# Two Fourier layers on one core: four splits in a row, image halves waited for apart, raw loads by ScalarE

## The reference

```
x = x + L0(gn(x))      # rfft2, keep 16x16 modes, mix channels per mode, irfft2; plus gn(x) @ skip + bias
x = x + L1(gn(x))      # rfft2, keep 32x32 modes, mix with fw1 and fw2, irfft2 = out; relu(out @ W + b + out)
```

## Time and profile before

| | |
|---|---|
| median of 3 runs | 2583.09 us (2573.79 to 2587.32) |
| profiled execution, its own time | 2586.72 us |
| its span | 2584.9 us |
| its mean granted clock of TensorE | 0.836 |
| busy, share of the span | TensorE 74%, VectorE 55%, ScalarE 44%, GpSimd 8% |
| bytes moved by DMA | 590.30 MB, mean 228 GB/s |

### The profile page before, as it was taken

One profiled execution on the slowest core, in us unless ns is written; L12 is line 12 of the kernel. 1 busy time (PEld: TensorE's weight loads), 2 busy tenths in 40 slices (PEclk: granted clock), 3 DMA queues, 4 the chain that ended last, 5 costly groups with the idle time before them and its releaser, 6 DMA issues. The chain is left out here.

```text
span 2584.9 us, 60445 instructions
## 1 busy us (share of the span) xinstructions
PE 1920.0 (74%) x24234; PEld 1537.6 (59%) x24234; DVE 1411.0 (55%) x2087; ACT 1145.1 (44%) x1884; POOL 194.5 (8%) x218
## 2 busy tenths in 40 slices
PE   4788887888389233323453699989999989999999
PEld 3566665667357232323343577777877777777877
DVE  5665665664144300000352576677777767777876
ACT  4544454553023200000232565556666556555665
POOL 0000000000100310110001120200102020201000
PEclk9999998999555555555676899999999999999999
DMA  7777676772664999999654487887878788878887
GB/s 274 237 221 221 222 229 204 231 238 87 153 83 67 193 232 232 233 234 223 168 179 176 130 285 261 286 287 238 279 255 302 257 288 271 294 267 266 275 285 274
DMA packets 239409, 590.30 MB, mean 228 GB/s; under 512 B 67302, under 2 KB 159938, under 8 KB 202306
## 3 DMA queue, kind: packets, MB, share of 16 engines
q1 hardware_dynamic: 203266, 570.90, 74.1%
q10 hardware_dynamic: 35072, 12.59, 2.4%
q0 software_dynamic: 768, 2.56, 0.3%
HBM read 380.99 MB, written 168.30 MB: 212 GB/s over the span
## 5 line engine op out<-in xcount | busy, mean ns | idle before, releaser
L1257 ACT ACTIVATE x_turned<-ps_xt 128x512 f16<-128x512 f32 x512 | 305.7, 597 | 422.8 <-PE ps_xt L1345 422.8
L1300 DVE TENSOR_TENSOR x_turned<-ps_xt,x_turned 128x512 f16<-128x512 f32 x512 | 350.6, 685 | 188.4 <-ACT x_turned L1257 169.9
L1389 PE MATMUL ps_y<-apply,x_turned 128*128 (+1 forms) x6144 | 436.5, 222 | 0.0
L1389 PEld LDWEIGHTS ps_y<-apply,x_turned 128*128 128x128 f16 x6144 | 385.9, 99 | 67.9 <-issue 5.2
L1345 PE MATMUL ps_xt<-c_eye,x_in 128*128 128x128 f32 x2048 | 321.6, 281 | 81.0 <-DMA x_in<-in_x 55.9
L221 DVE TENSOR_TENSOR parts<-stage,parts 128x1024 f16<-128x1024 f32 x256 | 304.3, 1220 | 127.5 <-ACT parts L145 126.8
L1321 DVE SCALAR_TENSOR_TENSOR y_out<-ps_y,relu 128x512 f32<-128x512 f32 x512 | 350.6, 685 | 30.2 <-PE ps_y L1389 12.7
L1267 ACT ACTIVATE relu<-ps_wave 128x512 f32<-128x512 f32 x512 | 303.1, 592 | 21.2 <-PE ps_wave L1375 21.1
L291 PE MATMUL row_ps<-parts,c_rows_dft 128*64 128x512 f16 x1536 | 215.2, 421 | 125.5 <-DVE parts L221 119.1
L145 ACT ACTIVATE parts<-stage 128x1024 f16<-128x1024 f32 x256 | 255.2, 1049 | 74.6 <-issue 37.2
L1345 PEld LDWEIGHTS ps_xt<-c_eye,x_in 128*128 128x128 f32 x2048 | 222.8, 144 | 84.8 <-DMA x_in<-in_x 45.7
(11 more groups left out here) (117 smaller groups left out, 2053.6 us busy)
## 6 DMA issues: line engine op xcount, KB each, us to landing
stage<-in_x SPq DMA_DIRECT2D x256, 512.0 KB, 4.6
x_in<-in_x SPq DMA_DIRECT2D x128, 1024.0 KB, 9.4
out_y<-y_out SPq DMA_DIRECT2D x128, 1024.0 KB, 4.8
fw_first<-in_fw SPq DMA_DIRECT2D x16, 2048.0 KB, 22.5
fw<-in_fw SPq DMA_DIRECT2D x16, 2048.0 KB, 24.7
raw<-mixed SPq DMA_DIRECT2D x16, 1024.0 KB, 6.8
planes_in<-planes SPq DMA_DIRECT2D x8, 1536.0 KB, 15.2
fw_first<-in_conv SPq DMA_DIRECT2D x8, 1024.0 KB, 16.0
```

The lines of the kernel that those rows point to most:

```text
L1257: nc.scalar.activation(turned[u % 2][:, 0, :, :], ps_turn[u % 2][:, :, :], ACT.Copy).then_inc(turn_high, 1)
L1300: nc.vector.tensor_tensor(v[:, 1, :, :], ps_turn[u % 2][:, :, :], v[:, 0, :, :], ALU.subtract).then_inc(turn_split, 1)
L1389: mm = nc.tensor.matmul(ps_y[u % 2][:, :, 2 * k:2 * k + 2], turned[u % 2][:, p, k, :], apply[:, bass.ds(b, 1), q, :, :].rearrange("p o c w ...
```

## The change

It has three parts. In `pass_1`, ScalarE and VectorE run split 3 of the next step right behind splits 1 and 2; before, ScalarE had the step's second turn eviction ahead of split 3, and VectorE its row eviction and its second turn eviction. Split 0 stays where it was, and the evictions keep their order. TensorE's row products of half 0 no longer wait for all four low parts of the step at their start: they wait for quads 0 and 1 ahead of the six matmuls of hh 0, and for quads 2 and 3 ahead of those of hh 1. In `project_1`, the loads of images 2 to 7 move from SyncE's queue to ScalarE, which issues them in step 1 of image b (for b+2) ahead of that step's eviction, behind the turn eviction of step 2; the wait on `combined` goes with them. The loads of images 0 and 1 stay with SyncE.

```
 ScalarE, pass_1                                 VectorE, pass_1
     split(nb, nt, 1)                                split(nb, nt, 1)
     split(nb, nt, 2)                                split(nb, nt, 2)
+    split(nb, nt, 3)                            +   split(nb, nt, 3)
     take_turn(b - 1, 2 * t + 1)                     take_rows(b, parity, t, lag)
-    split(nb, nt, 3)                                take_turn(b - 1, 2 * t + 1)
     take_modes (t == 6)                         -   split(nb, nt, 3)
```

```diff
             def row_products(b, t, half):
-                if half == 0:
-                    pe.wait_ge(low, (b * STEPS + t + 1) * QUADS + 2 * QUADS)
                 pe.wait_ge(rows_taken[half], b * STEPS + t + 1)
                 v = parts[t % 2]
                 n = 0
                 for hh in range(HALVES):
+                    if half == 0:
+                        pe.wait_ge(low, (b * STEPS + t) * QUADS + 2 * (hh + 1) + 2 * QUADS)
...
+        def load(eng, b):
+            v = raw[b % 2]
+            for f in range(2):
+                src = mixed[f, b].rearrange("r x y q w -> (x y) r (q w)")
+                eng.dma_start(v[:, f, :, 0:Q - 1, :, :].rearrange("p r k o w -> p r (k o w)"),
+                              src[0:P]).then_inc(landed[b % 2], 16)
+                eng.dma_start(v[0:K1, f, :, Q - 1, :, :].rearrange("p r o w -> p r (o w)"),
+                              src[P:, :, 0:2 * C]).then_inc(landed[b % 2], 16)
...
             for b in range(B):
-                if b + 2 < B:
-                    sp.wait_ge(combined, 4 * (b + 1))
-                    load(b + 2)
                 sp.wait_ge(out_taken, (b + 1) * STEPS)
...
                     act.wait_ge(stored[b % 2], 16 * STORES * (b // 2))
+                if s == 1 and b + 2 < B:
+                    act.wait_ge(combined, 4 * (b + 1))
+                    load(act, b + 2)
                 act.wait_ge(out_ready, n + 1)
```

More of the change, by code:

```diff
@@ L187, in image @@
                         split(nb, nt, 2)
+                    if ahead:
+                        split(nb, nt, 3)
                     if lag and 2 * t + 1 < TURN_STEPS:
                         take_turn(b - 1, 2 * t + 1)
-                    if ahead:
-                        split(nb, nt, 3)
                     if lag and t == 6:
@@ L946, in out_slots @@
             return [out[b % 2][:, h, part, :, q:q + STEP, :] for part in range(2)]
+        def load(eng, b):
[6 more added lines that the diff above has]
+                              src[P:, :, 0:2 * C]).then_inc(landed[b % 2], 16)
         @block.sync
         def _(sp):
[L950 to L957, removed]
             for b in range(min(B, 2)):
                 sp.wait_ge(cleared, b + 1)
-                load(b)
+                load(sp, b)
             for b in range(B):
-                if b + 2 < B:
-                    sp.wait_ge(combined, 4 * (b + 1))
-                    load(b + 2)
                 sp.wait_ge(out_taken, (b + 1) * STEPS)
```

## The result

The changed kernel takes 2484.69 us (median of 4 runs, 2476.86 to 2490.34), the kernel before beside it 2583.24. The ratio is 0.9621, 95% interval 0.9578 to 0.9664: 98 us less. I had predicted 2497, range 2472 to 2526. The profiled execution took 2479.07 us, 107.6 less than that of before.

The account below looks back on a forecast made before the run. The prediction took pass_1's turn steps as bound by a loop through three engines, column steps by TensorE. 53.2 + 11 + 22 + 0 = 86.2 us off 2586.7 gives 2500.5; the median lies 3.6 lower: 2497, range 2472 to 2526.

Parts of the forecast that it names:

- The loop: pass_1 turn steps: the period through three engines falls from 9.33 to 7.43 us, 53.2 us less over 28 steps.
- the added wait: pass_1 column steps: TensorE's extra wait has come true long before; cost taken as 0, at most 1.4 us.
- The clock: pass_1: smaller gaps ahead of TensorE's steps bring back three quarters of 30 us lost to lower granted clock, 22 us.
- My fear that step 0 would keep some: pass_1: step 0, with its 1.5 us gap, stays a place for the granted clock to fall.
- The jumps: pass_1 column stretches: two jumps of the image loop, about 3.2 us each, stay as they are.
- the clock keeps falling: Rival, pass_1: the clock dips come as often as now, so 2519 us; chance 0.14.
- Image 0: pass_1, first image: the same loop without turns, steps of about 6.0 us for 7.25, 11 us less.
- a second limit at 349 GB/s: pass_1, image 0: loads of 2.10 MB a step at a full DMA share hold the step at 6.0 us.
- project_1: Stage project_1: moving the raw loads to ScalarE gains 0 us, since stores and loads share busy DMA engines.
- raw loads pay: Rival, project_1: VectorE's waits for raw tiles go and become time saved, 23 us, so 2474 us; chance 0.10.

Follow-up runs that it names:

- split 1 first: The changed kernel with split 1 moved ahead of the first turn eviction on ScalarE and VectorE: 2468.84 us, ratio 0.9586.
- halved wait alone: The kernel before, with only row products of half 0 waiting for quads 0 and 1, then for 2 and 3: 2542.92 us, ratio 0.9859.
- order alone: The kernel before, with only split 3 moved right behind split 2 on ScalarE and VectorE, one wait for all four quads: 2519.09 us, ratio 0.9776.
- raw loads alone: The kernel before, with only the raw loads of project_1 moved to ScalarE: 2574.62 us, ratio 0.9988.
- wide stores: The changed kernel with project_1's seven large stores an image cut one per x, 32 partitions and all four planes each: 2435.38 us, ratio 0.9454.

## Why the prediction was right

**The loop.** Right, and nearly exact. Turn steps of 9.33 us became 7.48 (7.43 forecast); 28 of them give 1.85 x 28 = 51.8 us for 53.2. Of the 0.05 us missed, 0.03 are the estimate of where the second half of a row product begins: 0.67 us in, not 0.7; the other 0.02 stay open. Column steps kept their 8.48 us, so the added wait cost nothing there, as assumed. The same loop gave 8.67 and 8.13 for its two parts, and with split 1 first the step fell to TensorE's own work, which shows that ScalarE's first turn eviction stood in it.

**The clock.** The mechanism was right, and the term of 22 us too small: the turn stretches gained 79.0, less 51.8 is 27.2, of 30 that could come back. My fear that step 0 would keep some was wrong; the lower level remains at the two jumps of the image loop, where the column stretches with a jump have a granted clock of 0.91. The jumps did not stay at 3.2 us, as I had let them. The row product behind one:

```profile
205.25 2.77 PE L290 MATMUL row_ps<-parts,c_rows_dft 128*64 128x512 f16 x12 [4.54 <-issue]
```

The two jumps, 4.54 and 4.52 us for 3.19 and 3.16, cost about the 2.4 us that the column stretches lost. The halved wait alone has 4.52 and 4.47 us there, the order alone 2.86 and 2.98, and split 1 first, which has both, 3.13 and 4.09. So the halved wait is nearer to it than the order; the cause was not found. The rival that the clock keeps falling had 0.14 and is out.

**Image 0.** 12.7 us for 11. I had taken the loads as a second limit at 349 GB/s; they moved 368, and the steps were 6.01 us, as the loop has it (5.96, or 5.99 with the 0.67 of above). With a DMA share of 0.99 the loads had nothing to spare at that rate, so the two limits that I had put at 5.96 and 6.0 us do lie side by side.

**project_1.** Right that 23 us of waits for raw tiles were not 23 us of time: ScalarE's wait for stores took them over, and the raw loads alone measure 0.9988. That the narrow stores filled four DMA engines was an inference from a share of 0.25; the wide stores bear it out. The rival "raw loads pay" is out, but the term was some 3 us and not 0. Here the trace agrees with the sentence of the Trainium skill ("DMA: Bandwidth & Descriptors", section "Issuing engines are not separate DMA queues") that another issuer saves only issue time, and the 44 us that the stage lost with stores recut along another dimension agree with the rule of that page's section "Why a DMA increments its semaphore by 16 and not by 1" on how many engines a transfer is split over.

**What wasn't in the sum.** The tail of `pass_1` takes 14.5 us or 25 to 26 for the same matmuls, and `pass_2` took 1170.0 to 1181.0 us in the nine profiles though no kernel changed it. Both make the profiled pair differ by more (11.8 and 5.4 us). The medians, 98 us apart, are the fairer measure, and 12 us more than my 86. The clock (+5), image 0 (+2), `project_1` (+3), the loop (-1) and the jumps (-2) come to 7 of them. The other 5 are less than the 11 us by which the measured difference is uncertain, and what they are is not shown. The misses went both ways, so that the sum came this near owes a little to luck.

## What to carry to other kernels

Write down a loop through the engines' queues as offsets from one event, with the start of each instruction from one step of the timeline: moving one instruction then gives the new period to a few hundredths, and an end that is needed only by half of the consumer's work counts by that half. When a gap ahead of TensorE's work closes, look at the granted clock of that stretch too: here it gave back half as much again as the queue, and all of it had come back when the gap was 1.39 us and not yet 0.62. And a wait for a transfer that stands behind others in a queue says nothing about gain until the DMA share is read: a share that stays at a quarter while transfers are queued asks for another shape of the transfer, not another issuer.

## What the runs showed of the hardware

- A stretch of 128 float32 matmuls with TensorE busy throughout can stay at the lower clock to its end: 25.9 us at a granted clock near 0.5, against 14.5 at 1.00. In the kernel before, the level fell in the tail's first 4 us (0.71 there, 0.50 from then on) and did not rise again; with the halved wait alone and the order alone the tail took 25.2 and 25.5 us; in the other six profiles it took 14.5. What decides it was not found: kernels with the same code up to there showed both.
- The mean granted clock of the turn stretches was 0.90, 0.94, 1.00 and 1.00 with a gap of 2.59, 1.82, 1.39 and 0.62 us in each step. The gap and TensorE's busy share changed together, so these four kernels don't say which of them counts.
- Stores of 1.04 MB an image, nearly all in 1 KB pieces, went at 86 GB/s with x as the slowest dimension (4 or 3) of most of them. With 32 partitions as the slowest the stage took 44 us less, and ScalarE's wait for stored planes fell from 43.7 to 9.6 us.
